# Down-projection of layer 0: ten of a chunk's 33 tiles in three fast products, rounded and subtracted in pairs, instead of eight rounded one by one

## What is computed

```python
x  = L0_attn_x                                   # (32, 256, 128)
xn = layernorm(x)
# experts of layer 0: T = 8192 tokens, H = 128, E = 64 experts of I = 64, 8 of them with a weight per token
g = einsum('th,ehi->tei', xn, Wg)
u = einsum('th,ehi->tei', xn, Wu)
h = silu(g) * u * coef[:, :, None]
moe_out = einsum('tei,eih->th', h, Wd)
shared  = (silu(xn @ SWg) * (xn @ SWu)) @ SWd    # one expert more, of 128, that has no coef
x = x + attention0(xn) + moe_out + shared
x = x + attention1(layernorm(x)) + experts1(layernorm(x))
```

## Time and profile before

| | |
|---|---|
| median of 3 runs | 1709.21 us (1709.17 to 1712.31) |
| the profiled execution | 1711.61 us |
| its span | 1709.8 us |
| PE busy, share of the span | 1669.5 us, 98% |
| DVE busy | 1384.7 us, 81% |
| ACT busy | 876.0 us, 51% |
| POOL busy | 630.7 us, 37% |
| L763, plain down products | 408 tiles |
| L751, L752, L754 | 120 tiles |
| L1362, subtraction for the low part | x120, mean 893 ns |
| L1412, cast for the high part | x120, mean 617 ns |

### The profile page before, as it was taken

How to read it: one execution, slowest core, us unless ns; L and a number is a source line. 1 busy time by engine, 2 the same in 40 slices (tenths; PEclk the granted TensorE clock), 3 DMA queues, 4 the chain that set the end, 5 groups by cost and what they waited for, 6 DMA issues and landing times.

```text
span 1709.8 us, 24980 instructions
## 1 busy us (share of the span) xinstructions
PE 1669.5 (98%) x7140; PEld 1207.7 (71%) x7140; DVE 1384.7 (81%) x3683; ACT 876.0 (51%) x1579; POOL 630.7 (37%) x656
## 2 busy tenths in 40 slices
PE   6999999999999999999999999999999999999995
PEld 4667777777777777777777777777777776767773
DVE  5768888888979797979798988888888887565557
ACT  5546464646464646464555555454646454554431
POOL 4421252424242424233323233333323243567770
PEclk9999999999999999999999999999999999999997
DMA  8949464646373737373737374655546445678758
GB/s 220 197 108 253 102 188 104 179 107 183 98 181 100 190 97 202 97 199 84 197 95 194 86 176 106 147 135 124 158 99 177 89 121 156 209 258 271 233 172 313
DMA packets 172310, 273.93 MB, mean 160 GB/s; under 512 B 14280, under 2 KB 57288, under 8 KB 171920
## 3 DMA queue, kind: packets, MB, share of 16 engines
q1 hardware_dynamic: 163600, 254.63, 56.2%
q0 software_dynamic: 8576, 17.70, 3.3%
HBM read 202.15 MB, written 65.93 MB: 157 GB/s over the span
## 4 chain that ended last, share of the span: by engine, by line
PE 84%; DVE 5%; ACT 5%; issue 4%; DMA 1%; SPq 0%; DVEq 0%; POOL 0%; ACTq 0%; POOLq 0%
PE ps_y L763 18%; PE ps_up L703 8%; PE ps_up L705 7%; PE ps_up L704 7%; PE ps_gate L703 7%; PE ps_gate L705 7%; PE ps_gate L704 7%; PE ps_y L789 4%; PE ps_side L718 3%; DVE silu_h L979 2%; PE ps_side L812 1%; ACT L1401 1%; PE ps_side L906 1%; PE ps_y L754 1%; PE ps_y L752 1%
## 5 line engine op out<-in xcount | busy, mean ns | idle before, releaser
L979 DVE TENSOR_TENSOR silu_h<-ps_up,silu_h 128x512 f32<-128x512 f32 x618 | 421.3, 684 | 272.3 <-ACT silu_h L1401 227.6
L1401 ACT ACTIVATE silu_h<-ps_gate 128x512 f32<-128x512 f32 x618 | 365.8, 598 | 503.1 <-PE ps_gate L705 498.5
L763 PE MATMUL ps_y<-silu_h,w_dn 128*128 128x512 f32 x800 | 408.9, 593 | 0.8 <-DVE silu_h L967 0.8
L967 DVE TENSOR_TENSOR silu_h<-coef_b,silu_h 128x1024 f32<-128x1024 f32 x256 | 328.3, 1283 | 5.6 <-DMA coef_b<-coef_kept 4.4
L703 PE MATMUL ps_gate<-xnT,w_gu 128*128 128x512 f32 x528 | 309.4, 586 | 0.0
L703 PE MATMUL ps_up<-xnT,w_gu 128*128 128x512 f32 x528 | 212.8, 403 | 4.0 <-DVE silu_h L979 2.7
L705 PE MATMUL ps_gate<-xnT,w_gu 128*128 128x512 f32 x528 | 210.1, 398 | 0.0
L704 PE MATMUL ps_up<-xnT,w_gu 128*128 128x512 f32 x528 | 209.3, 396 | 0.0
L705 PE MATMUL ps_up<-xnT,w_gu 128*128 128x512 f32 x528 | 209.1, 396 | 0.0
L704 PE MATMUL ps_gate<-xnT,w_gu 128*128 128x512 f32 x528 | 208.9, 396 | 0.0
L1686 POOL TENSOR_TENSOR msg<-msg 128x512 f32<-128x512 f32 x48 | 68.7, 1431 | 314.5 <-ACT msg L1564 314.5
(11 more groups left out here) (279 smaller groups left out, 2857.1 us busy)
## 6 DMA issues: line engine op xcount, KB each, us to landing
coef_b<-coef_kept SPq DMA_DIRECT2D x254, 512.0 KB, 6.9
slots_x<-empty SPq DMA_DIRECT2D x15, 2080.0 KB, 12.5
w_block<-w_kept SPq DMA_DIRECT2D x45, 512.0 KB, 3.9
xs<-slots_x SPq DMA_DIRECT2D x37, 260.0 KB, 3.7
y_back<-y_kept SPq DMA_DIRECT2D x15, 512.0 KB, 7.0
w_down<-in_ffn_w SPq DMA_DIRECT2D x45, 128.0 KB, 3.7
w_raw<-in_ffn_w SPq DMA_DIRECT2D x33, 128.0 KB, 5.8
xres<-in_x SPq DMA_DIRECT2D x16, 256.0 KB, 3.1
```

The source lines that it names most:

```text
L763: eng.matmul(ps_y[:, :], down_of(j), silu_h[:, h_at(g)], start=j == 0, stop=last).then_inc(pe_down)
L967: eng.tensor_tensor(silu_h[:, s:s + 2], coef_b[:, q % COEF_RING, k:k + 2], silu_h[:, s:s + 2], ALU.mult).then_inc(dve_h)
L979: eng.tensor_tensor(silu_h[:, s], ps_up[g % 2][:, :], silu_h[:, s], ALU.mult).then_inc(dve_h1)
L1401: eng.activation(silu_h[:, s], ps_gate[g % 2][:, :], ACT.Silu).then_inc(act_silu)
```

## The change

Ten tiles of a chunk take the three fp32r products: 0, 1, 4, 5, 8, 9, 12, 13, 30 and 31 (`SPLIT_PAIRS`). The cast and the subtraction each take both tiles of a pair in one instruction of 1024 columns. `pair_round` stands on ACT at the beginning of step j + 3, j being the first tile of the pair, ahead of `silu`; `pair_rest` on DVE at the beginning of the same step. `h_hi` grows to two tiles. `h_lo` has no memory of its own any more: it lies over `silu_h`, so that the subtraction overwrites h with its low part. Tile 0 can now be a split one and then begins the accumulation in `ps_y`. On ACT `y_out` moves behind `silu` of its step. The raw down weights are loaded by ten DMAs in the order of the tiles in place of five; those of the ten split tiles wait in `rows1` and `yT`, and `split_down` makes their parts in two instructions on each engine. A gap of 32 bytes ahead of `counted` moves the tensors behind it.

```diff
-SPLIT_EACH = 4
-SPLITS0 = PAIRS0 // SPLIT_EACH
+SPLIT_PAIRS = (0, 4, 8, 12, 30)
+SPLIT_TILES = [j + k for j in SPLIT_PAIRS for k in range(2)]
+PLAIN_TILES = [j for j in range(TILES0) if j not in SPLIT_TILES]
+SPLITS0 = len(SPLIT_TILES)
+EARLY_HOME = 8
+RUNS = [(0, 2), (2, 4), (4, 6), (6, 8), (8, 10), (10, 12), (12, 14), (14, 30), (30, 32), (32, 33)]
...
+        at_h = ExitStack()
+        h_lo = sb("h_lo", [HBUFS, CHUNK], FP32R, within=at_h)
+        at_h.close()
         silu_h = sb("silu_h", [HBUFS, CHUNK])
-        h_hi = sb("h_hi", [CHUNK], FP32R)
-        h_lo = sb("h_lo", [CHUNK], FP32R)
+        h_hi = sb("h_hi", [2, CHUNK], FP32R)
...
+        sb("gap", [8])
         counted = sb("counted", [EXPERTS1, 16])
...
-            for n in range(SPLIT_EACH):
-                to = w_dn[:, n * SPLITS0:(n + 1) * SPLITS0] if n < SPLIT_EACH - 1 else w_dr
-                eng.dma_start(to, downs[n]).then_inc(w_dn_in[n], 16)
-            eng.dma_start(w_dn[:, (SPLIT_EACH - 1) * SPLITS0], ffn_w[PAIRS0, :, 2 * P:]).then_inc(w_dn_in[SPLIT_EACH], 16)
+            for n, (first, past) in enumerate(RUNS):
+                eng.dma_start(raw_downs(first, past), ffn_w[first:past, :, 2 * P:].rearrange("n p d -> p n d")).then_inc(w_dn_in[n], 16)
...
                 if split_h(g):
-                    n, k = split_before(g), j // SPLIT_EACH
-                    eng.wait_ge(dve_wds, 1)
+                    n, k = pairs_before(g), j % 2
+                    eng.wait_ge(dve_wds, 2)
                     eng.wait_ge(act_hhi, n + 1)
-                    eng.matmul(ps_y[:, :], w_ds[:, 0, k], h_hi[:, :], start=False, stop=False)
-                    eng.matmul(ps_y[:, :], w_ds[:, 1, k], h_hi[:, :], start=False, stop=False)
+                    if j == 0:
+                        eng.wait_ge(act_y, c)
+                    eng.matmul(ps_y[:, :], split_weights(0, j), h_hi[:, k], start=j == 0, stop=False)
+                    eng.matmul(ps_y[:, :], split_weights(1, j), h_hi[:, k], start=False, stop=False)
                     eng.wait_ge(dve_hlo, n + 1)
-                    eng.matmul(ps_y[:, :], w_ds[:, 0, k], h_lo[:, :], start=False, stop=False).then_inc(pe_down)
+                    eng.matmul(ps_y[:, :], split_weights(0, j), h_lo[:, h_at(g)], start=False, stop=False).then_inc(pe_down)
                     return
...
-            def h_rest(g):
-                n = split_before(g)
-                eng.wait_ge(act_hhi, n + 1)
-                if n > 0:
-                    eng.wait_ge(pe_down, split_tile(n - 1) + 1)
-                eng.tensor_tensor(h_lo[:, :], silu_h[:, h_at(g)], f32(h_hi[:, :]), ALU.subtract).then_inc(dve_hlo)
+            def pair_rest(g):
+                s = h_at(g - 1)
+                eng.wait_ge(act_hhi, pairs_before(g) + 1)
+                eng.tensor_tensor(h_lo[:, s:s + 2], silu_h[:, s:s + 2], f32(h_hi[:, :, :]), ALU.subtract).then_inc(dve_hlo)
...
-                if split_h(g - 3):
-                    h_rest(g - 3)
+                if split_pair(g - 2):
+                    pair_rest(g - 2)
...
-            def h_round(g):
-                n = split_before(g)
+            def pair_round(g):
+                n, s = pairs_before(g), h_at(g - 1)
                 eng.wait_ge(dve_h, scaled_before(g) + 1)
                 if n > 0:
-                    eng.wait_ge(pe_down, split_tile(n - 1) + 1)
-                eng.copy(h_hi[:, :], silu_h[:, h_at(g)]).then_inc(act_hhi)
+                    eng.wait_ge(pe_down, last_of_pair(n - 1) + 1)
+                eng.copy(h_hi[:, :, :], silu_h[:, s:s + 2]).then_inc(act_hhi)
...
+                if split_pair(g - 2):
+                    pair_round(g - 2)
+                if TILES_FIRST <= g < TILES + UNITS1:
+                    silu(g)
                 if 0 <= g - LAG0 < TILES and (g - LAG0 + 1) % TILES0 == 0:
                     y_out((g - LAG0 + 1) // TILES0 - 1)
-                if TILES_FIRST <= g < TILES + UNITS1:
-                    silu(g)
-                if split_h(g - 2):
-                    h_round(g - 2)
```

More of the change, by code:

```diff
@@ L1403, in split_down @@
             def split_down():
[L1404 to L1408 removed]
+                for n, (first, _) in enumerate(RUNS):
+                    if first in SPLIT_TILES:
+                        eng.wait_ge(w_dn_in[n], 16)
+                for n in range(2):
+                    eng.copy(w_ds[:, 0, EARLY_HOME * n:EARLY_HOME * n + w_dr[n].shape[1]], w_dr[n]).then_inc(act_wds)
+            def pair_round(g):
+                n, s = pairs_before(g), h_at(g - 1)
                 eng.wait_ge(dve_h, scaled_before(g) + 1)
                 if n > 0:
[L1411 to L1412 removed]
+                    eng.wait_ge(pe_down, last_of_pair(n - 1) + 1)
+                eng.copy(h_hi[:, :, :], silu_h[:, s:s + 2]).then_inc(act_hhi)
             def y_out(c):
@@ L1416, in y_out @@
                     eng.wait_ge(*done("yT", c - 1))
+                if c == 0:
+                    eng.wait_ge(dve_wds, 2)
                 eng.wait_ge(pe_down, (c + 1) * TILES0)
```

45 lines of the change are left out of this document (24 added, 21 removed).

## The result

The changed kernel took 1732.0 us (median of 4 runs, 1731.23 to 1733.15) against 1709.19 us for the kernel before on the same chip: a ratio of 1.0135, 95% interval 1.0122 to 1.0147. It is slower by 22.8 us, where 13.3 was forecast, and 1.0 us above the upper end of the range. The profiled execution took 1733.15 us, its span 1731.3 us, 21.5 us more than before's. The other 1.3 us of the 22.8 lie in how far the two profiled executions stand above their medians (2.4 us before, 1.15 now).

A forecast was written before the change was run, and what follows sets the result against it. PE's own work was taken to bound layer 0. Per chunk -0.32 - 0.2 + 0.27 + 1.2 = +0.95 us, times 14 is 13.3 us, on 1709.2 gives 1722.5 us; range 1704 to 1731, the forecast itself 1714 to 1731.

The forecast's parts named there:

- Rival 3: Pair (4, 5): POOL holds DVE's subtraction to its end, PE waits 0.8 us in each chunk, 1733.5 us; chance 0.08.
- part 1: Products on PE: two more split tiles a chunk save 2 x 0.16 = 0.32 us a chunk.
- part 2: Subtractions leave DVE at steps 18, 22, 26 and 30, so the wait at step 32 goes: -0.2 us a chunk.
- part 3: Steps 10 to 14: pair (8, 9) delays up(11), silu(13) and up(13) by 1.2 us, costing nothing yet.
- part 4: h_rest(11) goes, coef(13) meets POOL's addition instead; PE's wait at step 16 grows to 0.6 us: +0.27 us a chunk.
- 14 x 0.95: Sum over chunks 1 to 14 of the net loss of 0.95 us a chunk: 13.3 us.
- Part 6: Chunk 0's five more DMA issues, y_out behind silu and the gap: at nothing; 2.3 us once if uncovered, +-1 us for the gap.

The follow-up runs named there:

- runs 1: Changed kernel with pair (12, 13) moved to (24, 25): 1708.9 us, ratio 1.000 against the kernel before.
- 2: Changed kernel with pair (8, 9) moved to (24, 25), (12, 13) kept: 1704.5 us, ratio 0.9973 against the kernel before.
- runs 3: Changed kernel with pairs (8, 9) and (12, 13) moved to 22 and 26: 1701.8 us, ratio 0.9962 against the kernel before.
- 8: Changed kernel with split pairs at 0, 4, 26 and 30 alone, eight split tiles: ratio 0.9959 against the kernel before.
- Run 6: Kernel before with chunk 0's raw down weights in nine loads instead of five, tiles 0 to 7 first: ratio 1.0001 against the kernel before.

## Why the prediction was right in direction and short in size

**The mechanism held.** The low part of tile 12 is late behind the masks of step 14, because pair (8, 9) has pushed the chain; runs 1 and 2 show both halves. PE's loss there was forecast as a wait of 1.1 us and 0.1 for a late weight load: in the quiet chunks the low product begins 1.35 us behind its neighbour instead of 0.23 and is 0.1 us longer, 1.2 in all. (The 1.25 us of idle time in chunk 9 agree with that figure by chance, for they contain 0.3 us that the stretched k features add; quiet chunks show 0.96.) The losses at step 16 were summed to 1.8 us a chunk and are 1.7 in the quiet chunks. The forecast chunk, 88.95 + 0.95 = 89.9 us, is the quiet chunk of the changed kernel to 0.05 us; that is closer than the sum deserves, because it starts from a chunk 0.12 us longer than those it describes. The stretched instruction at step 14 is coef(13), as said.

**Rival 3 (pair (4, 5) held by POOL).** The meeting takes place, and in most chunks DVE wins it: 1.23 us for the subtraction, 2.58 for POOL's instruction. In chunks 1 and 2 DVE loses it, with 1.69 us and 0.3 us of the chunk. Even then it is held for some 0.47 us of POOL's 1.49 (an estimate: 1.69 less 1.22) and not to POOL's end; the prediction had read as much from the row of L1148. In no chunk does PE wait the 0.8 us that the rival wanted.

**The products (part 1).** -0.32 us a chunk forecast, 0.32 shown by runs 3 and 8.

**The wait at step 32 (part 2).** Forecast -0.2 us, and no wait is left there. The kernel before lost 0.26 us at it in chunk 9 but 0.11 in chunk 12 (late weight load included); at every other step the two chunks are alike, so this is why chunk 12 is the shorter one.

**The chain (part 3).** silu(13) was to move by 1.2 us; against the kernel before it moved by 1.32 or 1.83 us, by the race at pair (8, 9). What the prediction did not see: the new subtraction has POOL's sending of rows for a neighbour. It took the subtraction's length from a row where POOL was quiet.

**The wait at step 16 (part 4).** up(14) was to come 0.1 us later than before. It came 0.2 us later in the quiet chunks and 0.7 in the others. PE was not 0.16 us earlier by then: counted from step 10 it has won two tiles (8, 9) and lost two (7, 11). Its loss there is 0.5 us in a quiet chunk where 0.6 was said.

**Where the missing 8.2 us are.** The step that failed is the one from one chunk to the kernel, the term "14 x 0.95" of the sum: it took chunks 1 to 14 for alike and chunk 15 for unchanged, and had no price for the clock. In the spans: chunks 1 to 14 grew by 22.2 us, not 13.3. Of that 14 x 1.12 = 15.7 is the quiet chunk, 89.95 against 88.83 us (the kernel before's chunks 10 to 14 are shorter than its chunk 9, from which the sum started), less 0.5 for its longer ones among chunks 1 to 9: 15.2, which is 1.9 over the forecast. The k features beside the splitting of weights bring 8 x 0.3 = 2.4 us; the prediction had seen this one and put it, at half, into the upper end alone. The subtraction of (8, 9) beside the sending brings 2.4 us in five chunks, that of (4, 5) 0.6 in two. The clock after the wait in chunk 4 brings 1.6. Chunk 15, counted as unchanged, grew by 2.3: its tile 12 waits 1.92 us for the low part and a low clock follows again, where the kernel before waited 0.94 us two steps later, for up(16). Against that chunk 0 fell by 2.4 us and the part behind layer 0 by 0.6. The sum is 22.2 + 2.3 - 2.4 - 0.6 = 21.5 us.

**The range.** Its upper end held half of one of these collisions and no price at all for the clock. Collisions with POOL, the clock behind a wait of over a microsecond, and chunk 15 all point the same way, up. That the result lies only 1.0 us above the range is luck in part: which collisions a chunk has, and behind which waits the clock falls, changed from run to run.

**Part 6, at nothing.** Chunk 0 did not grow by the DMA issues, it became 2.4 us shorter. Run 6's trace points at the order of the loads; its whole time neither shows nor excludes that. The gap is within what a run can tell.

## What to carry over

A sum made in one chunk is good for the chunks like it; before it is multiplied, look for the chunks that have other work beside the same step (here a splitting of weights in 2 to 9, the last chunk, the first), and price each kind. Where an instruction is put at a new place, read what the other engines run beside that place, not only what stands ahead of it on its own engine. And two moves that are each nearly free can cost several times their sum when they draw on the spare time of the same chain: test them apart and together.
